# D times x scaled by ScalarE and added on VectorE, in place of TensorE's products with a diagonal matrix

## The reference, cut to what matters

```python
def step(h, t):
    dec, dtt, xt, bt, ct = t
    h = dec[..., None, None] * h + (dtt[..., None] * xt)[..., None] * bt[:, None, None, :]
    y = jnp.einsum('bhpn,bn->bhp', h, ct)
    return (h, y)
...
y = jnp.moveaxis(ys, 0, 1) + D[None, None, :, None] * xh
y = y.reshape(B, L, D_INNER) * jax.nn.silu(z)
return y @ out_proj_w
```

## Time and profile before

| what | value |
|---|---|
| time, median of 3 runs | 888.56 us (888.48 to 889.17) |
| the profiled execution's own time | 887.77 us |
| its span in the trace | 885.7 us |
| TensorE busy / weight load busy | 804.8 us / 661.7 us |
| VectorE, ScalarE, GpSimd busy | 644.8, 544.2, 291.6 us |
| granted TensorE clock, mean | 0.978 of full; 1.00 in the slices of the loop |

### The profile page before, as it was taken

The page is one execution under the profiler, slowest core; times in us unless marked ns, Lnnn a source line. Parts: engine busy times, 40 slices in busy tenths (PEclk is TensorE's granted clock), DMA queues, the critical chain, the costliest instruction groups (busy, mean ns, idle before and its releaser), DMA issues.

```text
span 885.7 us, 23129 instructions
## 1 busy us (share of the span) xinstructions
PE 804.8 (91%) x7312; PEld 661.7 (75%) x7312; DVE 644.8 (73%) x1681; ACT 544.2 (61%) x1210; POOL 291.6 (33%) x447
## 2 busy tenths in 40 slices
PE   4567999999999999999999999999999999999767
PEld 3445787878788787878778787878878787887656
DVE  5785877878777786877777787777777787776434
ACT  4636565757666575766766575776667576665312
POOL 3542232333433242343324233342324234332202
PEclk9788999999999999999999999999999999999988
DMA  7600000000000000000000000000000000000000
GB/s 253 163 1 14 2 6 19 7 17 0 22 0 5 17 5 17 3 19 0 5 17 5 17 5 17 0 19 3 5 17 5 17 3 19 0 6 10 10 1 10
DMA packets 17107, 16.77 MB, mean 19 GB/s; under 512 B 6322, under 2 KB 15416, under 8 KB 16824
## 3 DMA queue, kind: packets, MB, share of 16 engines
q1 hardware_dynamic: 17080, 16.43, 6.5%
HBM read 12.23 MB, written 4.19 MB: 19 GB/s over the span
## 4 chain that ended last, share of the span: by engine, by line
PE 57%; DVE 12%; issue 9%; POOL 8%; DMA 8%; ACT 3%; SPq 2%; POOLq 0%; DVEq 0%; ACTq 0%
PE bank L1360 26%; PE bank L1636 7%; POOL w_raw L546 7%; DVE xa L990 5%; PE bank L1528 5%; DMA tok<-tokens 5%; PE bank L1608 4%; PE bank L1517 3%; PE bank L1697 3%; PE bank L1588 3%; DMA wt_raw<-weights 2%; PE bank L1573 2%; PE bank L1597 2%; DVE w_raw L1257 2%; PE bank L1366 1%
## 5 line engine op out<-in xcount | busy, mean ns | idle before, releaser
L1047 DVE SCALAR_TENSOR_TENSOR mr<-er,gm 128x512 f32<-128x512 f32 x192 | 131.5, 707 | 34.7 <-ACT er L721 33.0
L721 ACT ACTIVATE er<-bank 128x512 f32<-128x512 f32 x192 | 109.5, 597 | 53.0 <-PE bank L1517 52.4
L1697 PE MATMUL bank<-w2t,w_raw 128*128 128x192 f32 x576 | 120.3, 332 | 10.0 <-ACT w_raw L780 7.4
L752 ACT ACTIVATE sg<-bank 128x256 f32<-128x256 f32 x96 | 36.9, 384 | 113.1 <-PE bank L1360 113.1
L1697 PEld LDWEIGHTS bank<-w2t,w_raw 128*128 128x128 f32 x576 | 90.1, 190 | 20.7 <-ACT w_raw L780 9.6
L797 ACT ACTIVATE sg<-bank 128x256 f32<-128x256 f32 x144 | 55.4, 385 | 79.1 <-PE bank L1360 77.1
L990 DVE SCALAR_TENSOR_TENSOR xa<-xr,cw_,xa 128x256 f32<-128x256 f32 x192 | 93.5, 495 | 2.6 <-ACT xa L641 0.6
L1218 DVE TENSOR_TENSOR w_raw<-sg,bank 128x256 f32<-128x256 f32 x144 | 60.1, 417 | 31.4 <-ACT sg L797 30.4
L1528 PE MATMUL bank<-mr,xd 128*32 128x128 f32 x1536 | 69.4, 286 | 12.0 <-DVE mr L1047 11.8
L1360 PE MATMUL bank<-x_h,wt_lo 128*128 128x256 f16 x288 | 79.2, 275 | 0.0
L1360 PE MATMUL bank<-x_h,w_lo 128*128 128x256 f16 x288 | 79.2, 275 | 0.0
(11 more groups left out here) (234 smaller groups left out, 2159.2 us busy)
## 6 DMA issues: line engine op xcount, KB each, us to landing
out<-w_raw SPq DMA_DIRECT2D x16, 192.0 KB, 2.0
w_raw<-weights SPq DMA_DIRECT2D x1, 1924.0 KB, 10.8
wt_raw<-weights SPq DMA_DIRECT2D x2, 962.0 KB, 16.5
pos<-position SPq DMA_DIRECT2D x16, 96.0 KB, 2.8
ri<-exponent_rows SPq DMA_DIRECT2D x4, 384.0 KB, 4.4
tok<-tokens SPq DMA_DIRECT2D x16, 70.0 KB
sums<-lj SPq DMA_DIRECT2D x16, 64.0 KB, 2.2
ri<-sums SPq DMA_DIRECT2D x64, 12.0 KB
```

The lines of the kernel that those rows point to most:

```text
L721: act.activation(er[:, r % NER], p_d[r % 2][:].rearrange("p (h i) -> p h i", h=HG), ACT.Exp)\
L1047: ve.scalar_tensor_tensor(mr[:, r % NER], er[:, r % NER], 1.0, gm[:, r // NQ, :].unsqueeze(1).to_broadcast([128, HG, Q]), ALU.min, ALU.mult)\
L1697: ins = pe.matmul(p_ex[e][:, b * D:(b + 1) * D], hh[:, e % NHH, b * Q:(b + 1) * Q], w2t[:, e, :], start=True, stop=True)
```

## The change

ScalarE no longer makes `skip`. In its place `skipped_x(c)` on ScalarE scales the three channel tiles of `xs` for both sequences (three ACTIVATE of 128x256, with D as the scale of each partition) into a new tile `xk`, once a chunk. VectorE gets `skip_added(c, b)`, which adds `xk` to `t1` in place (128x384), after `from_state` and before `scanned`, once for each sequence. TensorE's six products a chunk go, and the first products of `masked` now start the accumulation in `p_y`. Where a wait was for `yq_done` (TensorE has read `xs`), it is now for `xk_ready`.

```diff
@@ ScalarE
-            act.wait_ge(in_first, 48)
-            for k in range(KT):
-                act.activation(skip[:, k], idf[:], ACT.Copy, scale=dsk[:, k:k + 1]).then_inc(setup_a, 1)
...
@@ convolved_first, and the same in convolved_rest
-                    act.wait_ge(yq_done, c * NR)
+                    act.wait_ge(xk_ready, c)
...
+            def skipped_x(c):
+
+                act.wait_ge(xs_ready, c + 1)
+                act.wait_ge(xs_first, c + 1)
+                if later(c):
+                    act.wait_ge(t1_sum[1], c)
+                for k in range(KT):
+                    ins = act.activation(xk[:, k], xs[:, k], ACT.Copy, scale=dsk[:, k:k + 1])
+                ins.then_inc(xk_ready, 1)
...
@@ experts (ScalarE)
                         if e == 7:
+                            skipped_x(p)
                             b_on_tokens(p)
...
@@ VectorE
+            def skip_added(c, b):
+
+                ve.wait_ge(t1_ready[b], c + 1)
+                ve.wait_ge(xk_ready, c + 1)
+                ve.tensor_tensor(t1[:, b], t1[:, b], xk[:, :, b, :], ALU.add).then_inc(t1_sum[b], 1)
+
             def scanned(c, b):
 
-                ve.wait_ge(t1_ready[b], c + 1)
+                ve.wait_ge(t1_sum[b], c + 1)
...
@@ ramp (VectorE), and the same for chunk 0, sequence 1
                 new_state(0, 0)
+                skip_added(0, 0)
                 scanned(0, 0)
...
@@ body (VectorE)
                     masks(f, (3,))
                     from_state(f, 0)
                     masks(f, (4,))
+                    skip_added(f, 0)
...
                     from_state(f, 1)
+                    skip_added(f, 1)
                     scanned(f, 1)
...
@@ masked (TensorE)
-                                        mr[:, r % NER, heads.index(h), :], start=False, stop=(h % 2 == 1),
+                                        mr[:, r % NER, heads.index(h), :], start=(h % 2 == 0), stop=(h % 2 == 1),
...
@@ first_scan and second_scan (TensorE): the six calls skipped_x(b, k), as
-                skipped_x(0, 0)
                 masked(c, (0, 1))
...
-                skipped_x(0, 1)
                 masked(c, (2, 3))
...
-            def skipped_x(b, k):
-                pe.matmul(p_y[:, k * Q:(k + 1) * Q], skip[:, k], xs[:, k, b, :], start=True, stop=False,
-                          skip_group_check=True)
```

More of the change, by code:

```diff
@@ L132, in program @@
         dsk = sb("dsk", [128, KT])
-        skip = sb("skip", [128, KT, 128])
         spread16 = sb("spread16", [128, KT, 2, 128], F16)
@@ L167, in program @@
         zs = sb("zs", [128, KT, NB, Q])
+        xk = sb("xk", [128, KT, NB, Q])
         dx = sb("dx", [128, NB, NH])
@@ L288, in program @@
         t1_ready = [sem(f"t1_ready{b}") for b in range(NB)]
+        xk_ready = sem("xk_ready")
+        t1_sum = [sem(f"t1_sum{b}") for b in range(NB)]
         sn_done = [sem(f"sn_done{b}") for b in range(NB)]
@@ L838, in ramp @@
                 act.activation(warm[:, 1:2], mhalf[:, 0:1], ACT.Exp)
+                skipped_x(0)
                 b_on_tokens(0)
@@ L853, in ramp @@
                 gates(1, 0, p_pair)
+                skipped_x(1)
                 act.activation(warm[:, 3:4], mhalf[:, 0:1], ACT.Exp)
@@ L1302, in ramp @@
                 from_state(0, 1)
+                skip_added(0, 1)
                 scanned(0, 1)
@@ L1533, in first_scan @@
             def first_scan(c, between):
-                if not later(c):
-                    pe.wait_ge(setup_a, 1 + KT)
                 pe.wait_ge(eend_ready, c + 1)
@@ L1547, in first_scan @@
                 between()
-                skipped_x(0, 2)
                 masked(c, (4,))
@@ L1556, in second_scan @@
                 pe.wait_ge(y_sum[0], c + 1)
-                skipped_x(1, 0)
                 masked(c, (6, 7))
@@ L1563, in second_scan @@
                     project_in_x(p, p_d, (0, 1), c)
-                skipped_x(1, 1)
                 masked(c, (8, 9))
@@ L1568, in second_scan @@
                     project_in_x(p, p_d, (2, 3), c)
-                skipped_x(1, 2)
                 masked(c, (10, 11))
-            def skipped_x(b, k):
-                pe.matmul(p_y[:, k * Q:(k + 1) * Q], skip[:, k], xs[:, k, b, :], start=True, stop=False,
-                          skip_group_check=True)
             def state_read(c, b, p):
```

## The result

Before 887.66 us (median of 12 runs, 886.38 to 889.17), changed 890.38 us (12 runs, 888.54 to 895.05): ratio 1.0033 [1.0018, 1.0048], 2.9 us slower (0.0033 of 887.66). I had forecast 889.0 us within 884.8 to 893.0, with "within 0.2%" as the likeliest of the three, and slower at 0.28. The time lies in the range, but 0.1 us above the forecast's own 886.8 to 890.3, and the likeliest case did not come: the change is 0.33%. Part of the nearness is luck. The forecast stood on the median of three runs, 888.56; that of twelve is 887.66. The change was forecast as +0.4 us and measured as 2.7 (by the medians) to 2.9 (by the ratio). The profiled execution took 891.94 us, with a span of 890.1 (before 885.7).

The account below looks back on a forecast made before the run. TensorE's stops behind other engines' chains, not its work, were taken to bound the kernel. Store delay +1.6, ramp -0.8 and outer bodies -0.4 gave +0.4 us on 888.56: 889.0 us, range 884.8 to 893.0.

Parts of the forecast that it names:

- within 0.2%: Whole kernel: time stays the same, a change under 0.2% (1.8 us); chance 0.52, against faster 0.20 and slower 0.28.
- the forecast's own 886.8 to 890.3: Whole kernel: the band around the summed forecast of 889.0 us, given chance 0.52.
- What bounds the kernel: Loop pass: TensorE stops at embedding, second scan and pass end behind other engines' chains; all six products precede a stop.
- TensorE is the bound: Rival, whole kernel: all 96 calls of D's products are kept as gain, 20 us less, 869 us; chance 0.06.
- A call worth 0.21 us, only the first of six on a path: TensorE in a pass: each call costs 0.21 us; only the first scan's first call matters, through other engines.
- Addition of sequence 0, +0.08 to +0.12 us a pass: VectorE, first scan: `skip_added` delays the second half of `weighed_sum`, store and embedding; 13 times, +1.6 us.
- Sequence 1, "so 0": VectorE, second scan: 0.59 us addition, all but 0.2 hidden by `new_state`'s wait, the rest ending at `lj`'s slack; 0.
- ScalarE's scalings, 0: ScalarE: three scalings of 0.49 us each, covered by the waits at `bt` and expert 8's `sg`; 0.
- Ramp and outer bodies, -1.2 us: Outside the loop: ramp -0.8 us, first and last body with a scan -0.4 us.
- Store delayed in full: Rival, VectorE between unit 4's mask and `out_sum`: sequence 0's addition costs 0.3 to 0.44 us, 13 times; 892.5 us, chance 0.22.

Follow-up runs that it names:

- the kernel with sequence 1's calls back: Kernel before with sequence 0 in the new form, sequence 1 by TensorE's products, and SyncE loading tokens ahead of the store: 872.68 us, ratio 0.9842.
- sequence 0 alone: Changed kernel, but sequence 1 by TensorE's products as before; only sequence 0 goes by ScalarE and VectorE: 887.03 us, ratio 0.9999.
- one sequence each: Two kernels, each with one sequence in the new form and the other by TensorE's products: sequence 0 new 887.03 us, sequence 1 new 889.67 us.
- GpSimd held back: Changed kernel with GpSimd's first addition of the experts' shares waiting until `cw` is written: 886.69 us, ratio 1.0004.
- the addition moved: Changed kernel with `skip_added` of sequence 0 moved behind `new_state`, past the last `weighed_sum` and the splits: 887.54 us, ratio 1.0009.

## Why the prediction was right or wrong

**What bounds the kernel: right.** TensorE's idle time in a pass (mean of twelve) went from 1.65 to 2.53 us: at the embedding from 0.88 to 1.23, at the router from 0.26 to 0.48, and 0.18 that is new at the transposes of v. In the loop none shows at `xn`'s transposes, before or after, where the prediction had a wait too. Without any product of D the kernel gains 3 to 4 us, not 20; the rival "TensorE is the bound" is refuted.

**A call worth 0.21 us, only the first of six on a path: right.** 0.23 us a pass without the D term, and with the load ahead of the store the kernel with sequence 1's calls back has the same pass to 0.01 us. One thing that I said of it was wrong: TensorE's busy time should fall by 30 to 40 us, as the group's 38.9 us suggests. It fell by 10.9, and by 18.7 without the D term (786.1 us). The durations of a group overlap its neighbours; what a call adds between the starts of its neighbours (0.21 us, 20 us in all) is the better price.

**Addition of sequence 0, +0.08 to +0.12 us a pass: right.** I took 0.47 us of occupied time and the trace has 0.47; the second half of `weighed_sum` moved by 0.08 us behind what came from elsewhere, and sequence 0 alone lengthens a pass by 0.07 us, 0.9 us in all against the 1.6 of the sum.

**Sequence 1, "so 0": wrong, and this is the step that failed.** Its size was right: an addition of 0.59 us, 0.39 hidden by `new_state`'s wait, 0.20 left. The prediction let this 0.2 us run "on through the routing" to `lj`'s 0.4 us of slack as if its length stayed the same on the way. It grew to 0.62 us, since the shift put `sc` and `e_w` beside GpSimd instructions that they had missed. 0.27 us a pass came out, 3.5 us over 13 passes. With it in place of the 0, with 0.9 instead of 1.6 for sequence 0, and from the median of twelve runs, the sum is 887.7 + 0.9 + 3.5 - 1.2 = 890.9, against 890.38.

**The rule that was named and set aside.** The Trainium skill, page "SBUF — State Buffer", section Who interferes with whom, says that VectorE and GpSimd share a pair of ports, that the one that issues first keeps it for its whole instruction and the other is blocked, and that VectorE needs it for an instruction with two SBUF inputs, or for one like `tensor_scalar` in a two-port mode. I weighed it for the new addition alone, and wrote that "no row here puts a GpSimd instruction on a path beside it, so it moves no term of mine". That was true of the addition, but a moved instruction is a changed one too. The trace agrees with the rule in these places: `e_w` (two SBUF inputs) and `sc` (`tensor_scalar`) end 0.02 and 0.03 us behind the GpSimd instruction that was issued first, while `new_state` at 412.59, with one input in PSUM, keeps its 0.56 us beside the same instruction. Before, `e_w` missed it by 0.11 us, and `e_sum` paid instead (0.43 us, ending at 422.48, with GpSimd's addition over at 422.46), harmlessly, because of the slack at `lj`. One row does not fit "for its whole instruction" as recorded: GpSimd's decay of the state (shown at the end), issued 0.04 us behind a mask with two SBUF inputs that has 0.64 us to go, loses 0.30 us and not 0.64, and issued 0.34 us behind one, as before (441.32 against 440.98), it loses nothing. The last third of a microsecond of a mask's recorded time held up nobody. Rows of before would have told me: they show a `tensor_scalar` of 128x2 at 0.43 us beside GpSimd, and `e_w` 0.11 us ahead of the same addition.

**ScalarE's scalings, 0: right.** Of after:

```profile
L676 ACT ACTIVATE xk<-xs,dsk 128x256 f32<-128x256 f32 x48 | 20.9, 511 | 0.0
```

511 ns against the 490 taken, `sg` of expert 8 had still waited 0.58 us, and the run without scalings has the same time.

**Ramp and outer bodies, -1.2 us: open.** In the profiled execution `onehot` of chunk 2 came 3.6 us sooner (84.54 against 88.14), and the stretch behind the loop was longer. Both hang in part on the granted clock. Windows of before and of after, from 812 to 830 us, where the last scan ends (the granted clock is the figure behind the engines):

```profile
812.00:830.00 18.00, 15.49 (x146) 12.79 (x147) 11.77 (x38) 7.65 (x20) 6.31 (x7) 1.00 0.01 2
```

```profile
812.00:830.00 18.00, 15.28 (x122) 11.12 (x120) 12.68 (x40) 5.78 (x14) 4.57 (x5) 0.81 0.01 2
```

The chains show what it does to the same 40 products, first before, then after:

```profile
817.91 4.37 PE bank L1360 x40
```

```profile
819.66 6.55 PE bank L1382 x40
```

In the ramp it is the other way: six products of the output projection take 1.92 us before and 0.97 after. So one execution can't price these parts. From the medians less 13 times the pass, the part outside the loop changed by -1.9 us in the changed kernel, -1.0 without the D term, -1.4 and -1.3 with one sequence each, -1.2 without scalings, and by nothing in the kernel with GpSimd held back and in that with the addition moved. The last two have the changed kernel's ramp, and the intervals of the ratios are 1.7 to 3.5 us wide, so these numbers neither confirm -1.2 nor refute it. On the clock: of the 13 profiled executions, five have a stretch at half speed in the last scan, and behind the last `onehot` they take 135.1 to 138.3 us, the other eight 134.2 to 134.9. The five are among the seven kernels with both sequences in the new form. The kernel without D, whose TensorE is busy less still, has none in its one execution, so the rows don't tie it to a lower load alone; the cause stays open.

**The rivals.** "Store delayed in full" gave 892.5 us for another reason than the one that holds: the second half of `weighed_sum` is 0.34 us later, within its 0.3 to 0.44, but 0.26 of it was there at the pass's first `weighed_sum`. The measured 890.38 lies between it and the forecast.

## What to carry to other kernels

When a change shifts a stream by a fraction of a microsecond, slack further on covers the shift only if nothing on the way changes its length. Look for short VectorE instructions on SBUF that start just ahead of, or just behind, a GpSimd instruction of 1 us, and price each at the rest of that instruction (here that held to 0.03 us for the three small ones). The cure can be a wait added on GpSimd. And before taking work from the busiest engine, ask which instruction sets its stops: here one order of two DMAs gave 10 us, and all the products of D 3 to 4 us.

## What the runs showed of the hardware

- A 128x16 `SCALAR_TENSOR_TENSOR` of 0.17 us took 0.77 us, a 128x16 `TENSOR_SCALAR` of 0.18 us took 0.49, and one of 70x256 went from 0.35 to 0.61 and 0.98 us, all by where they started relative to a GpSimd `TENSOR_TENSOR` of 1.00 us, which itself kept its 1.00 us.
- It goes the other way too. GpSimd's decay of the state lasts 1.34 us in the changed kernel, where it starts 0.04 us behind a mask of VectorE (439.75, 0.68 us), and 1.04 with the addition of sequence 0 moved away, where it starts 0.35 us behind the mask. From the kernel after:

```profile
439.79 1.34 POOL L483 TENSOR_TENSOR state<-state,ends 128x384 f32<-128x384 f32 x1 [1.95 <-PE bank L1390]
```

- In the same stage, the last scan, the granted clock was 1.00 in one execution (2.4 GHz throughout) and 0.81 in the other (partly at 1.2 GHz), though TensorE waited for `x_h` there in both. It costs 2.18 us on one chain of 40 products.
